# Second edge layer of a two-layer graph network: steps written out, one table word a step, landings passed on later

## The reference

```python
# x [50000, 256]; src, dst [50000] (sorted by dst); edge_type_8 in 0..7
h = jnp.maximum(_layernorm(x), 0.0)
xt = jnp.einsum('ni,rio->rno', h, weight)             # 8 relations
messages = xt[edge_type, dst]
out = segment_sum(messages, src, 50000)
x = x + relu(out + bias)

h = jnp.maximum(_layernorm(x), 0.0)
h_self, h_neigh = h @ W_self, h @ W_neigh
h_sparse = the 32 largest of each row of h_neigh, zero elsewhere
summed = segment_sum(h_sparse[src], dst, 50000)       # 50000 edges
deg = segment_sum(1, dst, 50000)
return x + h_self + summed / maximum(deg, 1)[:, None]
```

## Time and profile before

| | us |
|---|---|
| runs, median of 3 | 3609.3 (3604.76 to 3609.43) |
| the profiled execution | 3607.24, span 3605.5 |
| granted TensorE clock in it, mean | 0.904 |
| second edge layer, first matmul to last add | 2990.4 to 3601.9 |

### The profile page before, as it was taken

One profiled execution on the slowest core, in us unless ns is written; L12 is line 12 of the kernel. 1 busy time (PEld: TensorE's weight loads), 2 busy tenths in 40 slices (PEclk: granted clock), 3 DMA queues, 4 the chain that ended last, 5 costly groups with the idle time before them and its releaser, 6 DMA issues.

```text
span 3605.5 us, 69112 instructions
## 1 busy us (share of the span) xinstructions
PE 2593.9 (72%) x10738; PEld 1677.9 (47%) x10739; DVE 3119.8 (87%) x13785; ACT 2257.1 (63%) x6394; POOL 2450.8 (68%) x1732
## 2 busy tenths in 40 slices
PE   2665666767788888888677777777777765766676
PEld 1224655555566666666333333333333334555454
DVE  8998788888899999999699999999999995666666
ACT  3994233333333333333588888888888867777787
POOL 0003877767787777777688888888888855656665
PEclk9997888888999999999899899998988988889999
DMA  9601466666555555555344444444444437777776
GB/s 368 248 0 48 83 123 144 147 143 149 110 108 104 104 100 103 105 102 100 109 173 164 182 166 171 178 163 177 173 164 182 166 121 244 257 242 258 247 251 218
DMA packets 308041, 576.38 MB, mean 160 GB/s; under 512 B 32095, under 2 KB 188034, under 8 KB 307982
## 3 DMA queue, kind: packets, MB, share of 16 engines
q1 hardware_dynamic: 212366, 419.40, 33.2%
q0 software_dynamic: 95616, 156.31, 22.3%
HBM read 316.70 MB, written 258.88 MB: 160 GB/s over the span
## 4 chain that ended last, share of the span: by engine, by line
DVE 50%; issue 21%; PE 11%; DMA 8%; POOL 4%; DVEq 3%; ACT 2%; POOLq 0%; ACTq 0%; SPq 0%
DVE zone_c L1176 7%; DVE w L1176 7%; DVE best L1169 6%; DVE zone_c L1204 5%; DMA agg<-msg,sidx 5%; PE banks L1569 5%; DMA w<-hs,gidx 3%; PE banks L1469 2%; DVE zone_c L858 2%; DVE zone_c L1049 2%; DVE zone_c L1047 2%; DVE stats L893 2%; DVE zone_c L860 2%; DVE zone_c L1051 2%; POOL rows_in L653 2%
## 5 line engine op out<-in xcount | busy, mean ns | idle before, releaser
L1541 PE MATMUL banks<-w,hT 128*128 128x512 f32 x1568 | 795.4, 666 | 199.8 <-ACT hT L1321 195.1
L665 POOL DMA_INDIRECT agg<-msg,sidx x400 | 665.3, 1663 | 206.4 <-issue 111.9
L653 POOL DMA_INDIRECT rows_in<-in_x,gidx x400 | 421.8, 1054 | 435.7 <-DVE gidx L909 305.3
L1541 PEld LDWEIGHTS banks<-w,hT 128*128 128x128 f32 x1568 | 325.7, 213 | 613.3 <-issue 500.6
L1204 DVE SCALAR_TENSOR_TENSOR zone_c<-banks,rdeg,zone_c 128x256 f32 x784 | 379.4, 484 | 245.8 <-PE banks L1569 201.0
L1569 PE MATMUL banks<-w,zone_c 128*128 x1568 | 428.1, 429 | 208.4 <-DVE zone_c L1204 99.5
L732 POOL DMA_INDIRECT w<-hs,gidx x392 | 371.3, 947 | 230.3 <-DMA w<-hs,gidx 90.6
L1411 PE MATMUL banks<-pick,h 128*128 128x128 f32 x1600 | 287.1, 307 | 311.8 <-ACT h L1220 218.8
L1469 PE MATMUL banks<-w,hT 128*128 x1600 | 481.1, 429 | 18.3 <-issue 17.1
L1238 ACT COPY msg<-banks 128x256 f32<-128x256 f32 x400 | 148.0, 370 | 510.6 <-PE banks L1480 497.3
L1569 PEld LDWEIGHTS banks<-w,zone_c 128*128 128x128 f32 x1568 | 316.1, 212 | 320.6 <-issue 275.2
(11 more groups left out here) (233 smaller groups left out, 5841.6 us busy)
## 6 DMA issues: line engine op xcount, KB each, us to landing
out_rows<-zone_c SPq DMA_DIRECT2D x196, 512.0 KB, 2.7
agg<-bias SPq DMA_DIRECT2D x2, 25344.0 KB, 97.3
zone_c<-agg SPq DMA_DIRECT2D x98, 512.0 KB, 5.4
hs<-zone_c SPq DMA_DIRECT2D x98, 512.0 KB, 3.6
zone_c<-out_rows SPq DMA_DIRECT2D x98, 512.0 KB, 6.0
rows_in<-in_x SPq DMA_DIRECT2D x97, 512.0 KB, 4.6
keyrow<-key_rows SPq DMA_DIRECT2D x100, 320.0 KB, 4.0
zone_c<-bucket_rows SPq DMA_DIRECT2D x28, 448.0 KB
```

What stands on the lines that cost most here:

```text
L653: pool.indirect_dma_start(out=rows_in[p][:, j, :], out_offset=None, in_=x[:, :], in_offset=bass.IndirectOffsetOnAxis(ap=gidx[p][:, j:j + 1 ...
L665: pool.indirect_dma_start(out=agg[:, :], out_offset=bass.IndirectOffsetOnAxis(ap=sidx[p][:, j:j + 1], axis=0), in_=msg[p][:, j * D:(j + 1) ...
L1541: last = mm(bank[4 + j][:, :], hT[p][:, c, j * P:(j + 1) * P], w1[:, c, :], start=(c == 0), stop=(c == KC - 1))
```

## The change

It touches the second edge layer alone, and the tables for it:

- The loops of ACT, PE and DVE over steps are written out: all 784 steps stand in the program, and semaphore values are constants in place of register expressions.
- DVE loads 28 words for 28 steps, where it loaded 32 for 16: one word a step, 256 times the block's number. The offset in `y` is that word modulo 32 x 256, the block's number is the word divided by 256. It waits for `y_ready` each 14 steps, not each 8.
- PE loads 32 words for 28 steps (28 offsets, 4 values of `arrived`), where it loaded 20 for 16. It waits for `arrived` each 7 steps, not each 4, for the last tile of the seven; for `hot1_done` each 2 steps.
- ACT makes two `near` matrices with two activations of 128 columns and turns both into one-hots with one of 256 columns. `near` has 4 buffers of two; `hot1` has 8 slots as before, released in twos.
- POOL passes a landing on behind the gather five later (`LATE` 5), with eight semaphores `gathered1`. The copy of the list comes at `k == 5`.
- The tables `place` and `fetch` are built with fewer operations.

```diff
-GROUP = 16
-HALF_GROUP = 8
+GROUP = 28
+HALF_GROUP = 14
+FETCHED = 7
 QUARTERS = 4
+LANDINGS = 8
...
-        HOTS = 8
-        near = view(zone_c, 0, [4, P])
-        hot1 = view(zone_c, 4 * P, [HOTS, P])
+        HOTS, PAIR, NEARS = 8, 2, 4
+        near = view(zone_c, 0, [NEARS, PAIR * P])
+        hot1 = view(zone_c, NEARS * PAIR * P, [HOTS, P])
...
-            LATE = 3
+            LATE = 5
...
-                ).then_inc(gathered1[k % B], 16)
+                ).then_inc(gathered1[k % LANDINGS], 16)
...
-                        relay1((k - LATE) % B, i * (RING // B) + (k - LATE) // B + 1)
+                        relay1((k - LATE) % LANDINGS, i * (RING // LANDINGS) + (k - LATE) // LANDINGS + 1)
...
-                last_of_quarter = grouped(tile_of[0:1, :])[:, :, GROUP // QUARTERS - 1:GROUP:GROUP // QUARTERS]
-                v.tensor_scalar(fetch[0:1, :, GROUP:], last_of_quarter, float(TILES - 1), float(RING), ALU.min, ALU.add)
-                v.tensor_copy(place[0:1, :, GROUP:], grouped(node_of[0:1, :]))
-                v.tensor_copy(path_i[0:1, 0, :], tile_of[0:1, :])
-                link(v.tensor_scalar(path_i[0:1, 1, :], node_of[0:1, :], 0.0, None, ALU.add))
+                last_fetched = grouped(tile_of[0:1, :])[:, :, FETCHED - 1:GROUP:FETCHED]
+                v.tensor_scalar(fetch[0:1, :, GROUP:], last_fetched, float(TILES - 1), float(RING), ALU.min, ALU.add)
+                v.tensor_scalar(place[0:1, :, :], grouped(node_of[0:1, :]), float(D), None, ALU.mult)
+                link(v.tensor_copy(path_i[0:1, 0, :], tile_of[0:1, :]))
                 link(v.tensor_scalar(path_i[0:1, 0, :], path_i[0:1, 0, :], RING - 1, None, ALU.bitwise_and))
-                link(v.tensor_scalar(path_i[0:1, 1, :], path_i[0:1, 1, :], YR - 1, None, ALU.bitwise_and))
-                v.tensor_scalar(fetch[0:1, :, 0:GROUP], grouped(path_i[0:1, 0, :]), float(D), None, ALU.mult)
-                link(v.tensor_scalar(place[0:1, :, 0:GROUP], grouped(path_i[0:1, 1, :]), float(D), None, ALU.mult))
+                link(v.tensor_scalar(fetch[0:1, :, 0:GROUP], grouped(path_i[0:1, 0, :]), float(D), None, ALU.mult))
...
-            def add_steps(i):
+            def add_steps(i, half):
                 _, words = nc.values_load_multi_w_load_instructions(
-                    place[0:1, bass.ds(i, 1), :].rearrange("o g w -> o (g w)"), engines=[mybir.EngineType.DVE],
+                    place[0:1, bass.ds(i * 2 + half, 1), :].rearrange("o g w -> o (g w)"),
...
-                    to, node = y_cols[:, bass.ds(words[k], D)], rdeg[:, bass.ds(nodes[k], 1)]
+                    s, at = i * (2 * GROUP) + (half * GROUP + k), half * GROUP + k
+                    at_row = nc.s_assert_within(words[k] % (YR * D), 0, (YR - 1) * D,
+                                                skip_runtime_bounds_check_because=KNOWN_WORDS)
+                    node = nc.s_assert_within(words[k] // D, 0, TILES - 1,
+                                              skip_runtime_bounds_check_because=KNOWN_WORDS)
+                    to = y_cols[:, bass.ds(at_row, D)]
                     if k % HALF_GROUP == 0:
-                        last = nc.s_assert_within(words[GROUP + k + HALF_GROUP - 1], 0, TILES - 1)
-                        dve.wait_ge(y_ready, last // B + 1)
-                    dve.wait_ge(steps1, i * GROUP + (k + 1))
...
+                        last = nc.s_assert_within(words[k + HALF_GROUP - 1], 0, (TILES - 1) * D)
+                        dve.wait_ge(y_ready, last // (B * D) + 1)
+                    dve.wait_ge(steps1, s + 1)
...
-            add_steps(0)
-            with dve.Fori(1, STEPS1 // GROUP) as i:
-                add_steps(i)
+            for i in range(STEPS1 // (2 * GROUP)):
+                for half in range(2):
+                    add_steps(i, half)
...
+            def hot_pair(q, k):
+                wait_from(act, steps1, q * PAIR + (PAIR - HOTS), q, HOTS // PAIR)
+                act.wait_ge(near1, q + 1)
+                nc.scalar.activation(hot1[:, k * PAIR:(k + 1) * PAIR, :].rearrange("p k c -> p (k c)"),
+                                     near[:, k % NEARS, :], ACT.Relu, bias=ones[:, 0:1], scale=-1.0
                                      ).then_inc(hot1_done, 1)
...
-                    if k % (GROUP // QUARTERS) == 0:
-                        pe.wait_ge(arrived, nc.s_assert_within(words[GROUP + k // QUARTERS], 1, TILES + RING))
-                    pe.wait_ge(hot1_done, i * GROUP + (k + 1))
...
+                    if k % FETCHED == 0:
+                        pe.wait_ge(arrived, nc.s_assert_within(words[GROUP + k // FETCHED], 1, TILES + RING))
+                    if k % PAIR == 0:
+                        pe.wait_ge(hot1_done, i * (2 * GROUP // PAIR) + (at // PAIR + 1))
```

More of the change, by code:

```diff
@@ L346, in graph_layers @@
         w0_flat = w0[:, :, :, :].rearrange("p r c d -> p (r c d)")
-        path_i = view(w0_flat, 0, [2, STEPS1], I32)
-        place = view(zone_b, 0, [STEPS1 // GROUP, 2 * GROUP], I32)
-        fetch = view(zone_b, 2 * STEPS1, [STEPS1 // GROUP, GROUP + QUARTERS], I32)
+        path_i = view(w0_flat, 0, [1, STEPS1], I32)
+        place = view(zone_b, 0, [STEPS1 // GROUP, GROUP], I32)
+        fetch = view(zone_b, STEPS1, [STEPS1 // GROUP, GROUP + GROUP // FETCHED], I32)
         tile_last = sb("tile_last", [1, NB], I32)
@@ L429, in graph_layers @@
         top_stored = pair("top_stored")
-        gathered1 = [sem(f"gathered1_{j}") for j in range(B)]
+        gathered1 = [sem(f"gathered1_{j}") for j in range(LANDINGS)]
         hist_hot = sem("hist_hot")
@@ L766, in _ @@
             for t in range(TILES - LATE, TILES):
-                relay1(t % B, t // B + 1)
+                relay1(t % LANDINGS, t // LANDINGS + 1)
         @block.vector
@@ L1184, in _ @@
             node_over(dve)
-            KNOWN_WORDS = "the tables hold offsets of ring slots and row blocks that the path bounds by its length"
-            def add_steps(i):
+            KNOWN_WORDS = "the table holds 256 times the row block of a step, bounded by the number of blocks"
+            def add_steps(i, half):
                 _, words = nc.values_load_multi_w_load_instructions(
-                    place[0:1, bass.ds(i, 1), :].rearrange("o g w -> o (g w)"), engines=[mybir.EngineType.DVE],
-                    min_val=0, max_val=(YR - 1) * D, skip_runtime_bounds_check_because=KNOWN_WORDS)
-                nodes = [nc.s_assert_within(w, 0, TILES - 1, skip_runtime_bounds_check_because=KNOWN_WORDS)
-                         for w in words[GROUP:]]
+                    place[0:1, bass.ds(i * 2 + half, 1), :].rearrange("o g w -> o (g w)"),
+                    engines=[mybir.EngineType.DVE], min_val=0, max_val=TILES * D,
+                    skip_runtime_bounds_check_because=KNOWN_WORDS)
@@ new lines, in add_steps @@
+                    to = y_cols[:, bass.ds(at_row, D)]
+                    if k % HALF_GROUP == 0:
+                        last = nc.s_assert_within(words[k + HALF_GROUP - 1], 0, (TILES - 1) * D)
+                        dve.wait_ge(y_ready, last // (B * D) + 1)
+                    dve.wait_ge(steps1, s + 1)
+                    ins = v.scalar_tensor_tensor(to, bank[at % 8][:, 0:D], rdeg[:, bass.ds(node, 1)], to,
+                                                 ALU.mult, ALU.add)
+                    if s:
+                        ins._wait_ge(summed, s)
@@ L1336, in _, with near_pair @@
             node_over(act)
[L1338 to L1347, removed]
+            def near_pair(q, k):
+                wait_from(act, hot1_done, q - NEARS + 1, q, NEARS)
+                for j in range(PAIR):
+                    last = nc.scalar.activation(near[:, k % NEARS, j * P:(j + 1) * P], iota_f[:, 0:P], ACT.Abs,
+                                                bias=minus_key[:, bass.ds(q * PAIR + j, 1)])
+                last.then_inc(near1, 1)
+            def hot_pair(q, k):
[3 more added lines that the diff above has]
+                                     near[:, k % NEARS, :], ACT.Relu, bias=ones[:, 0:1], scale=-1.0
                                      ).then_inc(hot1_done, 1)
+            PAIRS, TURN = STEPS1 // PAIR, HOTS // PAIR
             act.wait_ge(tables_ready, 5)
[L1351 to L1362, removed]
+            near_pair(0, 0)
+            for q in range(PAIRS):
+                if q + 1 < PAIRS:
+                    near_pair(q + 1, (q + 1) % TURN)
+                hot_pair(q, q % TURN)
         @block.tensor
@@ L1554, in _, with merge_steps @@
             node_over(pe)
-            def merge_steps(i):
+            def merge_steps(i, half):
                 _, words = nc.values_load_multi_w_load_instructions(
-                    fetch[0:1, bass.ds(i, 1), :].rearrange("o g w -> o (g w)"), engines=[mybir.EngineType.PE],
-                    min_val=0, max_val=(RING - 1) * D,
+                    fetch[0:1, bass.ds(i * 2 + half, 1), :].rearrange("o g w -> o (g w)"),
```

(18 more changed lines are left out.)

10 lines of the change are left out of this document (2 added, 8 removed).

## The result

The changed kernel takes 3510.16 us (median of 4 runs, 3506.64 to 3515.34) against 3608.23 us, a ratio of 0.9731 (0.9714 to 0.9748): 98 us faster, 30 us more than forecast, inside the range. The profiled execution took 3515.3 us, 91.9 less than that of before; it was the slowest of the four runs, so 5 of the 30 us are spread between runs and not the merge.

What follows compares the result with a forecast made beforehand. DVE with its register loads was taken as the bound, 602 of the merge's 611.5 us. POOL's 516 plus 25 made 541, -70.5; with +4 start, +1.5 end, -2 tables, 3607.2 became 3540 us, range 3505 to 3600.

Steps and rivals of the forecast that it cites:

- The needs: Each engine's own time in the merge: POOL 516, DVE 501, DMA 486, PE 468, ACT 388 us.
- the surcharge of 25 us: Added to POOL's 516 in the merge for three close needs and late landings: a third of 90.6 us, less overlaps.
- the end's 1.5: End of the merge: seven steps instead of four hang on the last tile, +1.5 us.
- A's own range: Case A, the merge as summed, 3540 us: 3510 (nothing added) to 3575 us (twice as much stays); chance 0.62.
- DVE's need: DVE in the merge: 406.6 us of adds plus 27 gaps of 3.5 us at loads, 501 us.
- hardly a fixed part: Register loads on DVE and PE: cost goes by the word, 0.110 and 0.107 us, so 28 words take 3.06 us.
- Rival E: DVE's extra register operations put its step at 0.6 us or more: 3580 to 3600 us or no change; chance 0.08.
- ACT in pairs: ACT in the merge: 0.99 us a pair, 388 us in all, under DVE with 0.495 us a step.
- The start: Before the first matmul: the first seven steps ask for tile number 3, passed on behind gather number 8, +4 us.
- The tables: Building the tables on DVE: a copy, a mask, a conversion and one multiplication go, -2 us.
- rival B: DMA in the merge: more in flight makes landings later, so transfers replace the waits, 3584 us; chance 0.14.
- Rival C: Hand-over from POOL starves PE: each of 28 groups loses 1.5 us over A, 3582 us; chance 0.06.
- Rival D: Written-out code in the merge: some 20 unhidden instruction refills of 5.5 us, 110 us, 3650 us; chance 0.07.

Runs made afterwards that it cites:

- rolled_third: The changed kernel with PE's and DVE's steps in loops of 56 again, on the chip of 3605 us: 0.9745 of the kernel before.
- lean_pool: The changed kernel with POOL's four words of tile_last loaded one by one, on the chip of 3605 us: 0.9747 of the kernel before.
- half_gathers: The changed kernel with every second tile's gather left out, on the chip of 3659 us: 3478.0 us, 0.9505 of the kernel before.
- single_hots: The changed kernel with one-hots made one by one again, on the chip of 3676 us: 3630.7 us, 0.9874 of the kernel before.
- before_again: The kernel before, unchanged, run again on a slower chip, one with stalls: 3659 us.
- after_again: The changed kernel, unchanged, run again on the same chip as the kernel before at 3659 us: ratio 0.9863.

## Why the prediction was right, and where its terms were off

**The bound before** holds, read from the trace: DVE with its loads, 602 of 611 us. In all 48 gaps the next add starts 0.64 us behind the end of the load, filled with DVE's own register work to within 0.05, so PE fills none of them; inside the groups DVE waits 10 us in all. That DVE's loads, not its adds, were the movable part fits the changed kernel's trace, whose adds are as before (0.52 us a step) and whose gaps fell from 195 to 78 us in all. How much of the 93 us would come from the loads alone, and how much needed `LATE` 5, no run on a chip without stalls shows.

**The new bound.** The needs gave POOL 516 as the largest, and POOL's gathers span 516.4. What was mis-sized is the surcharge of 25 us: three needs within 6% of each other were to get in each other's way, with a third of the landing waits left. None was left (13.0 us, longest 0.3), and the merge took 518.3. With the end's 1.5, which lies in it, that is 24 of the 25 us by which the forecast was too high, the difference of 92 to 67. A third of 90.6 was also too much on its own terms, as 26 of the 90.6 were the usual gaps, counted already in 1.25 a gather.

That 516 met 516.4 is in part luck. POOL's program needs 511 at most (rolled_third) and 499 to 505 without its waits for PE, so some 11 to 17 us of the 516 were waiting, of the kind that the surcharge was for. The lower end of A's own range was summed wrongly as well: with nothing added, 3607.2 - 95.5 + 3.5 is 3515, not 3510.

That POOL's pace, and not DVE's, sets the merge is read from three traces without stalls: DVE's adds and gaps take 488, 506 and 484 us (changed kernel, rolled_third, lean_pool), the gathers 516.4, 510.9 and 511.5, and the merge 516.6, 512.8 and 511.1. On one chip, 22 us more of DVE's own work changed it by less than 2. No run makes POOL alone faster, so this isn't shown by experiment. half_gathers takes away POOL's work and DMA traffic together and shows what is under them: 490 us.

**DVE's need**: forecast 501, and 490 where it is the bound. A word cost 2.44/28 = 0.087 us (PE: 2.68/32 = 0.084), not 0.110; this price was taken from the loads of before and came out a fifth too high. No price of a word is fixed: the loads of 28 words took from 1.85 to 3.72 us in one trace. Nor does "hardly a fixed part" hold for POOL, where one word took 0.31 us and four 0.34. Two register operations a step were forecast at 0.1 to 0.3 and cost 0.09 in the fused one, and one plain of 0.04; hidden, as forecast. Rival E is out. Not foreseen was the 0.18 us at the second wait of a group, where 0.04 is usual, 28 times, 4 us.

**ACT in pairs** start 0.99 us apart:

```profile
3111.80 0.49 ACT L1349 ACTIVATE zone_c<-zone_c,ones 128x256 f32<-128x256 f32 x1
3112.20 0.68 ACT L1342 ACTIVATE zone_c<-iota_f,minus_key 128x128 f32<-128x128 f32 x2
3112.79 0.49 ACT L1349 ACTIVATE zone_c<-zone_c,ones 128x256 f32<-128x256 f32 x1
```

Forecast 0.99. Whether the pairs were needed, single_hots tells only for a chip with stalls: 0.9874 against 0.9863 on another such chip, no difference that can be told.

**The start** cost 2.2 us, not 4: PE began at 2991.6, after eight gathers, so its first seven steps seem to have asked for tile number 2, not 3. **The tables** gave nothing, where 2 us were booked: DVE's block was shorter, but the first search for the 32 largest waits for data behind it. It starts 1.1 us earlier, and DVE was already 1.4 us earlier ahead of the tables (1740.01 for 1741.38).

**DMA** at 0.90 and 290 GB/s was forecast rightly (0.9, 283) and did not bind, as POOL never waited for a landing: rival B is out. **Rival C** is out as a loss of 1.5 us a group, though its sign is there: PE waits 105.1 us for POOL's passing, up from 77.4 in the earlier trace rows. POOL itself waits only 12 us for PE beyond the usual gaps, so this is mostly PE's slack; the lower clock behind such waits, seen above, is its price. **Rival D**, code read once: 0.6 MB of instructions came in during the merge on the two instruction queues, and on the first chip PE's waits show none for issue. On the contrary, on chips with stalls the written-out code is what wins.

What no rival had: that the kernel before itself is 50 to 70 us slower in three of the five comparisons, and the change worth 1.4% and not 2.7% there.

## What to carry to other kernels

Where several engines feed each other through rings, take the largest of their own needs as the time and add little for their meeting; here, with needs of some 499 to 505 us (POOL) and 484 to 506 (DVE), the merge took 511 to 517. A gap that every instruction has is no waiting: take it off before booking a wait as a saving. Count register loads and register arithmetic as an engine's own work when it has a step under a microsecond: the page doesn't call them busy, and the loads alone were 49 x 3.52 = 172 of DVE's 611 us. And when a run with one part undone gives a number that fits no theory, run the two kernels themselves on the same chip before believing it.

## What the runs showed of the hardware that I had not expected

- In three of the five comparisons, each on a chip of its own as far as is known, the engines' queues stall for about 0.7 us at a time (longest plain register operations 714 and 727 ns where 45 and 32 are usual) in this merge. Ahead of 2960 us before_again, after_again and half_gathers have one register operation over 0.4 us each, and none over 0.45. The merge of the kernel before takes 670 us from first to last add with the stalls, not 610. With half the gathers left out, they are all but gone on the same chip, though the DMA engines are no less busy. Their cause is open.
- The time to load words into registers isn't constant: the medians come to 0.110 us a word for 32 words on DVE before and 0.087 for 28 after, 0.107 (20 words) and 0.084 (32) on PE. On POOL four words took 0.34 us and one 0.31, so there nearly all of it is a fixed part.
- A gather of 128 rows of 1 KB is 0.95 us on POOL and 0.30 us to the next, with the DMA engines' share at 0.77 in the merge before and at 0.90 after.
- After 3.21 us without work PE ran at a granted clock of 0.57, and the steps behind it came 0.85 us apart on DVE where 0.52 is usual.
